# Three tables of places changed in the cross layers of a fused scan network on one Trainium2 core

## The chip, the cores and the metric

The kernel runs on one core of one Trainium2 chip. The metric is the device time of one execution in microseconds (us), lower is better. Its five engines run side by side, each its own instructions in order: TensorE (PE in the rows, PEld its weight loads), VectorE (DVE), ScalarE (ACT), GpSimd (POOL) and SyncE (SP), which here only issues DMAs. Semaphores order them among each other.

## The reference

The input x has shape (4, 32, 32, 96): 4 images, 1024 positions, 96 channels. Four layers follow each other, each as x = x + layer(group_norm(x)). Layers 0 and 3 (L0 and L3, the cross layers) are four-direction selective scans, layer 1 is a stencil of products ("motif"), layer 2 a one-direction selective scan behind a 3x3 convolution. The change touches only the code that L0 and L3 share. Cut to what matters, such a layer computes

```
xz = x @ in_proj.T                       # 2 x 192 channels: xin and z
xs = [rows order, columns order, and both reversed](xin)        # 4 directions
dts, Bs, Cs = x_proj[k] @ xs[k]          # ranks 12, 16, 16
delta = softplus(dt_proj[k] @ dts + bias)
h_t = exp(delta_t * A) * h_{t-1} + delta_t * B_t * u_t          # 16 states a channel
y   = sum over states of C_t * h_t + D * u
y   = layernorm over the 192 channels of the sum over directions
out = (y * silu(z)) @ out_proj.T
```

## The kernel before

A cross layer works through 8 turns, two for each of the 4 images: number 2b with the rows order (r = 0), number 2b + 1 with the columns order (r = 1). A turn has 48 tiles, indexed t = 0 to 47, in 16 groups g of three tiles: a group is one pair of states (states p and p + 8 on the two halves of the partitions) of one direction, its three tiles c = 0, 1, 2 are the three blocks of 64 of the 192 channels. Every tile is 128 x 1024.

One tile is: ACT takes the decay exp(delta * A) (L843); DVE multiplies du by the B row (L1007, "inject"; for c = 2 POOL does it, L897) and runs the scan (L1028); POOL multiplies the state by the C row (L910, "read"), with three read buffers; PE adds the two state halves into y_ps (L696). In each group ACT also copies the B row from SBUF to PSUM for the two DVE injects (L828, copy_b). It stands in front of the decay of the group's second tile.

SP loads the B and C rows of group g + 1 in iteration g of its loop (L568 and L577; load_c waits until POOL has read group g - 1). Beside that it makes the doubled copies of delta and du that a block of channels needs (copy_block, L549 and L550, four DMAs of 256 KB a block). Three blocks (q = 0, 1, 2, the first half of the next turn) are copied in the iterations that COPY_ABOVE lists, one row for r = 0 and one for r = 1; the other three at the iterations of COPY_BELOW. SP issues in order, so copies and what they wait for stand ahead of later row loads.

Between the tiles lie side products, which finish the image before (FINISH) and prepare the next turn (PREPARE). All go through a single PSUM bank side_ps, so a side product can't start before the one before it has been taken out. The tables give for each half of a side product (tile at which PE issues it, tile at which ACT takes it, tile at which DVE uses it). PE issues a side product ahead of the y addition of the tile with that index, ACT takes it behind the decay of its tile, DVE uses it ahead of the inject of its tile. The keys that matter:

- ("cent", j), the centred products: y minus its channel mean, for the layer norm. cent 0 has two halves of 4 matmuls in the trace, cent 1 is one product of 8 (lines L668 and L666). DVE multiplies the gate by it (L980), ACT squares it (L774) and so frees side_ps. They exist only in turns with r = 0 and b > 0: 3 turns in each of the two layers, 6 in all. Below, product 1, 2 and 3 are cent 0 half 0, cent 0 half 1 and cent 1.
- ("sum", j): the finished delta of block pair j, used by DVE (L976).

ACT_SOFTPLUS places the five ACT passes of the softplus for each j by tile: exp (L784), log (L789), one (L794), less (L797), relu (L800). Between less and relu comes the subtraction "gap" with both operands in SBUF, on POOL (L882) at tiles of POOL_GAP or on DVE (L994) at tiles of DVE_GAP. For j = 2 it is on DVE: tile 38 for r = 0, tile 33 for r = 1. At a given tile ACT does its decay first, then the takes, then the softplus passes. The copy_b of a group comes before the decay of its second tile.

Of the kernel before, what the change touches and what calls it, by code (L numbers as in the profile page):

```python
# [128 lines left out]
def motif_layer(nc, x_cm, g_cm, ident, cols, ahead):  # L129
# [5 lines left out]
    with cleared(nc) as (ctx, sems):  # L135
# [79 lines left out]
        def _(dve):  # L215
# [82 lines left out]
            for k in range(banks_out):  # L298
# [13 lines left out]


FINISH = [
    {("cent", 0): ((0, 5, 3), (2, 7, 6)),
     ("cent", 1): ((4, 9, 8),),
     ("var", 0): ((10, 14, None), (11, 15, None)),
     ("out", 0): ((14, None, 18), (15, None, 19))},
    {("z", 0): ((37, 40, None), (38, 41, None)),
# [22 lines left out]
     ("sum", 2): ((33, 37, 37), (36, 40, 39))}]  # L342
ACT_SOFTPLUS = [
    {("exp", 0): 23, ("log", 0): 23, ("one", 0): 25, ("less", 0): 25, ("exp", 1): 26, ("log", 1): 26,
     ("one", 1): 28, ("relu", 0): 29, ("less", 1): 31, ("relu", 1): 34, ("exp", 2): 36, ("log", 2): 36,
     ("one", 2): 36, ("less", 2): 36, ("relu", 2): 40},
    {("exp", 0): 16, ("log", 0): 16, ("one", 0): 18, ("less", 0): 20, ("relu", 0): 22, ("exp", 1): 25,
     ("log", 1): 27, ("one", 1): 27, ("less", 1): 29, ("exp", 2): 29, ("relu", 1): 31, ("log", 2): 31,
     ("one", 2): 31, ("less", 2): 31, ("relu", 2): 34}]
POOL_GAP = [{30: 1}, {20: 0, 27: 1}]  # L350
DVE_GAP = [{26: 0, 38: 2}, {33: 2}]
# [4 lines left out]
FILL, FILL_FIRST = 1, 2  # L356
FILL_AFTER = {(("var", 0), 1): 0, (("out", 0), 0): 0, (("out", 0), 1): 0, (("sum", 2), 1): 0,
              (("sum", 1), 0): 0}
COPY_BELOW, COPY_ABOVE = (1, 2, 3), ((13, 13, 15), (9, 9, 13))


def side_uses(r, finish):
# [1442 lines left out]
```

## Time and profile before

| what | value |
|---|---|
| median of 3 runs | 3565.45 us (3564.26 to 3565.74) |
| the profiled execution | 3555.9 us, span 3554.1 us |
| POOL busy / DVE busy | 2788.5 us (78%) / 3031.2 us (85%) |
| PE busy / ACT busy | 2451.9 us (69%) / 2049.0 us (58%) |
| reads L910 | 768 of 2387 ns mean |
| injects on POOL L897 | 256 of 2358 ns mean |
| scans L1028 | 768 in three groups of 2286, 2287 and 2271 ns mean |
| mean granted TensorE clock | 0.814 of full speed |

The profile is of one execution. A number in brackets behind an instruction is the idle time of its engine ahead of it, with the instruction or DMA that ended it. The time of a row is its start in us from the start of the span. In a chain of tiles an engine that is never idle sets the pace, and the idle time of the others costs nothing.

### The profile page before, as it was taken

To read this page: it belongs to the slowest core of one execution; us is meant where nothing else is said; L and a number is where in the kernel's file an instruction comes from. 1 tells how busy PE (TensorE), PEld (TensorE's weight loads), DVE (VectorE), ACT (ScalarE), POOL (GpSimd) and SP (SyncE) were. 2 spreads that over 40 slices of the span, in tenths; PEclk is the share of its full clock that TensorE was granted. 3 is DMA by queue.
4 is the path that set the end of the run, shared out by engine and by line. 5 is a ranking of instruction groups with operands and counts; after the bars stand their busy time and mean duration, and the time that the engine had idled before them with its cause. 6 is when DMAs were issued, how large, how long until landed. Compare 5 with 4: busy or idle time off the path is not lost. (4 is left out here: it accounts for less than half of the span.)

```text
span 3554.1 us, 27486 instructions
## 1 busy us (share of the span) xinstructions
PE 2451.9 (69%) x5948; PEld 618.1 (17%) x5948; DVE 3031.2 (85%) x1958; ACT 2049.0 (58%) x2262; POOL 2788.5 (78%) x1188
## 2 busy tenths in 40 slices
PE   5767676677677667335677776766776777768776
PEld 2111111111121111111111112111111111111111
DVE  1899999999999998685989841999999999999995
ACT  3566665757565665304656524657575656666564
POOL 0899999989998999003666622999899989999995
PEclk9787888879788878657788778778897888788788
DMA  2655556654755465103442402566537555655663
GB/s 49 160 138 145 140 136 157 153 131 116 180 132 142 124 155 127 30 0 90 120 106 80 119 11 68 145 161 149 141 111 178 140 136 125 159 136 136 148 152 91
DMA packets 140881, 437.19 MB, mean 123 GB/s; under 512 B 33909, under 2 KB 34619, under 8 KB 140395
## 3 DMA queue, kind: packets, MB, share of 16 engines
q1 hardware_dynamic: 140714, 435.58, 50.4%
q14 instruction: 137, 1.12, 0.1%
q8 instruction: 30, 0.49, 0.1%
HBM read 307.56 MB, written 6.82 MB: 88 GB/s over the span
## 5 line engine op out<-in xcount | busy, mean ns | idle before, releaser
L910 POOL TENSOR_TENSOR L_read<-L_state,L_c_rows 128x1024 f32<-128x1024 f32 x768 | 1818.7, 2387 | 115.9 <-DVE L_state L1028 70.5
L696 PE MATMUL L_y_ps<-L_read,L_fold 128*64 128x512 f32 x3072 | 990.5, 743 | 467.7 <-POOL L_read L910 467.5
L897 POOL TENSOR_TENSOR L_state<-L_du,L_b_rows 128x1024 f32<-128x1024 f32 x256 | 603.7, 2358 | 27.4 <-POOL L_read L910 4.1
L1028 DVE TENSOR_TENSOR_SCAN L_state<-L_decay,L_work_ps 128x1024 f32<-128x1024 f32 x256 | 585.3, 2286 | 27.7 <-DVE L_work_ps L1007 4.0
L843 ACT ACTIVATE L_decay<-L_delta,L_a_neg 128x1024 f32<-128x1024 f32 x512 | 584.1, 1141 | 16.1 <-DVE L_state L1028 9.2
L1028 DVE TENSOR_TENSOR_SCAN L_state<-L_decay,L_row_ps 128x1024 f32<-128x1024 f32 x256 | 585.4, 2287 | 8.8
L1028 DVE TENSOR_TENSOR_SCAN L_state<-L_work_ps,L_state 128x1024 f32<-128x1024 f32 x256 | 581.4, 2271 | 13.4 <-POOL L_state L897 8.2
L843 ACT ACTIVATE L_work_ps<-L_delta,L_a_neg 128x1024 f32<-128x1024 f32 x256 | 285.8, 1116 | 460.1 <-DVE L_state L1028 459.1
L1007 DVE TENSOR_TENSOR L_work_ps<-L_du,L_row_ps 128x1024 f32<-128x1024 f32 x256 | 314.3, 1228 | 196.2 <-issue 145.7
L696 PEld LDWEIGHTS L_y_ps<-L_read,L_fold 128*64 128x64 f32 x3072 | 183.4, 154 | 1214.7 <-POOL L_read L910 901.6
L1558 POOL TENSOR_TENSOR L_read<-L_state,L_c_rows 128x1024 f32<-128x1024 f32 x96 | 237.6, 2475 | 164.7 <-DVE L_state L1664 138.8
L828 ACT COPY L_row_ps<-L_b_rows 128x1024 f32<-128x1024 f32 x256 | 260.1, 1016 | 156.1 <-DVE L_state L1028 101.0
L1007 DVE TENSOR_TENSOR L_row_ps<-L_du,L_row_ps 128x1024 f32<-128x1024 f32 x256 | 309.4, 1208 | 0.0
L1664 DVE TENSOR_TENSOR_SCAN L_state<-L_decay,L_b_ps 128x1024 f32<-128x1024 f32 x96 | 219.5, 2286 | 3.3
L668 PE MATMUL L_side_ps<-g_cm,L_w_u 96*128 (+1 forms) x216 | 162.4, 843 | 44.9 <-ACTq L763 26.0
L668 PE MATMUL L_side_ps<-L_dbl,L_w_dt 128*128 128x512 f32 x216 | 142.6, 747 | 45.7 <-ACT L_delta L755 37.6
L1642 DVE TENSOR_TENSOR L_b_ps<-L_du,L_b_ps 128x1024 f32<-128x1024 f32 x96 | 117.2, 1221 | 59.8 <-DMA L_du<-L_du_a 41.8
L1354 PE MATMUL L_y_ps<-L_read,L_fold 128*64 128x512 f32 x384 | 126.3, 736 | 51.5 <-POOL L_read L1558 48.1
L1507 ACT ACTIVATE L_decay<-L_delta,L_a_neg 128x1024 f32<-128x1024 f32 x96 | 109.1, 1144 | 64.0 <-DVE L_state L1664 41.2
L1536 POOL TENSOR_TENSOR L_l_a<-L_more,L_l_a 128x1024 f32<-128x1024 f32 x4 | 9.4, 2362 | 169.7 <-ACT L_more L1436 169.6
L759 ACT COPY L_delta<-L_side_ps 128x512 f32<-128x512 f32 x108 | 62.7, 581 | 131.9 <-DVE L_u L976 55.6
L882 POOL TENSOR_TENSOR L_y_b<-L_more,L_y_b 128x1024 f32<-128x1024 f32 x10 | 23.5, 2354 | 121.7 <-ACT L_more L797 121.7
(326 smaller groups left out, 2933.5 us busy)
## 6 DMA issues: line engine op xcount, KB each, us to landing
L_b_rows<-L_bc_dram SPq DMA_DIRECT2D x580, 256.0 KB, 4.2
L_c_rows<-L_bc_dram SPq DMA_DIRECT2D x580, 256.0 KB, 4.0
L_delta<-L_delta SPq DMA_DIRECT2D x204, 256.0 KB, 5.2
L_du<-L_du SPq DMA_DIRECT2D x140, 256.0 KB, 5.6
L_du<-L_u SPq DMA_DIRECT2D x64, 256.0 KB, 6.0
L_bc_dram<-L_dbl SPq DMA_DIRECT2D x40, 128.0 KB, 3.4
L_delta<-L_delta_a SPq DMA_DIRECT2D x16, 256.0 KB, 4.4
L_du<-L_du_a SPq DMA_DIRECT2D x16, 256.0 KB, 5.0
```

Source lines behind the costliest of these rows:

```text
L668: m = nc.tensor.matmul(side_ps[0:rows, :], part[0], part[1], **flags)
L696: m = nc.tensor.matmul(y_to(c, o, i), fold[:, :], y_half(t, o, i), start=first, stop=last, skip_group_check=True)
L828: nc.scalar.copy(row_ps[:, :], b_rows[:, g % 2, :]).then_inc(b_ready, 1)
L843: nc.scalar.activation(to[:, :], delta2[:, d * NBLK + c, :], ACT.Exp, scale=a_neg[:, o * 2 + d, c, p:p + 1]).then_inc(decay_ready, 1)
L897: nc.gpsimd.tensor_tensor(state[:, last, :], du2[:, d * NBLK + last, :], b_rows[:, g % 2, :], ALU.mult).then_inc(injected_c, 1)
L910: nc.gpsimd.tensor_tensor(read[:, t % READS, :], state[:, t % STATES, :], c_rows[:, g % 2, :], ALU.mult).then_inc(multiplied, 1)
L1007: nc.vector.tensor_tensor(to[:, :], du2[:, d * NBLK + c, :], row_ps[:, :], ALU.mult).then_inc(injected, 1)
L1028: nc.vector.tensor_tensor_scan(state[:, c, way], by[:, way], fed[:, way], 0.0, ALU.mult, ALU.add).then_inc(scanned, 1)
L1354: m = nc.tensor.matmul(y_ps[quarter(i), c, :], fold[:, :], read[:, t % READS, s], start=t < NBLK, stop=t >= NT - NBLK, skip_group_check=True)
L1558: nc.gpsimd.tensor_tensor(read[:, t % READS, :], state[:, t % STATES, :], c_rows[:, p % 2, :], ALU.mult).then_inc(multiplied, 1)
L1642: nc.vector.tensor_tensor(to[:, :], du2[:, slot(number, c), :], row[:, :], ALU.mult).then_inc(injected, 1)
L1664: nc.vector.tensor_tensor_scan(state[:, t % STATES, :], decay[:, t % DECAYS, :], fed[:, :], 0.0, ALU.mult, ALU.add).then_inc(scanned, 1)
```

## The change

Three edits, all in tables of tile numbers; no instruction is added or removed, and both programs have the same number on each engine.

1. FINISH[0]: on PE product 1 goes from ahead of the y addition of tile 0 to ahead of that of tile 1, product 2 from tile 2 to tile 3; product 3 stays at 4. DVE uses product 1 at tile 4 instead of 3, product 3 at 7 instead of 8. ACT takes product 3 at tile 8 instead of 9.
2. ACT_SOFTPLUS, block pair j = 2: for r = 0 exp goes from tile 36 to 34, log to 35, one and less to 37; for r = 1 exp goes from 29 to 28 and log from 31 to 29.
3. COPY_ABOVE: for r = 0 from iterations (13, 13, 15) to (12, 13, 14), for r = 1 from (9, 9, 13) to (10, 11, 12).

```
-    {("cent", 0): ((0, 5, 3), (2, 7, 6)),
-     ("cent", 1): ((4, 9, 8),),
+    {("cent", 0): ((1, 5, 4), (3, 7, 6)),
+     ("cent", 1): ((4, 8, 7),),
...
-     ("one", 1): 28, ("relu", 0): 29, ("less", 1): 31, ("relu", 1): 34, ("exp", 2): 36, ("log", 2): 36,
-     ("one", 2): 36, ("less", 2): 36, ("relu", 2): 40},
+     ("one", 1): 28, ("relu", 0): 29, ("less", 1): 31, ("relu", 1): 34, ("exp", 2): 34, ("log", 2): 35,
+     ("one", 2): 37, ("less", 2): 37, ("relu", 2): 40},
     {("exp", 0): 16, ("log", 0): 16, ("one", 0): 18, ("less", 0): 20, ("relu", 0): 22, ("exp", 1): 25,
-     ("log", 1): 27, ("one", 1): 27, ("less", 1): 29, ("exp", 2): 29, ("relu", 1): 31, ("log", 2): 31,
+     ("log", 1): 27, ("one", 1): 27, ("exp", 2): 28, ("less", 1): 29, ("log", 2): 29, ("relu", 1): 31,
...
-COPY_BELOW, COPY_ABOVE = (1, 2, 3), ((13, 13, 15), (9, 9, 13))
+COPY_BELOW, COPY_ABOVE = (1, 2, 3), ((12, 13, 14), (10, 11, 12))
```

On PE, at the start of an r = 0 turn that finishes an image, before (the rows with L_cent_w and L_less_w are a centred product, L696 a y addition, L703 the skip term):

```order
L661 ISA
L668 MATMUL L_side_ps<-L_y_a,L_cent_w 128x512
L668 MATMUL L_side_ps<-L_y_b,L_less_w 128x512
L692 REGISTER_ALU
L693 ISA
L696 MATMUL L_y_ps<-L_read,L_fold 64x512 x2
L692 REGISTER_ALU
L693 REGISTER_ALU
L696 MATMUL L_y_ps<-L_read,L_fold 64x512 x2
L661 REGISTER_ALU
L668 MATMUL L_side_ps<-L_y_a,L_cent_w 128x512
L668 MATMUL L_side_ps<-L_y_b,L_less_w 128x512
```

and in the changed kernel, from the same place:

```order
L693 ISA
L696 MATMUL L_y_ps<-L_read,L_fold 64x512 x2
L649 REGISTER_ALU
L661 ISA
L668 MATMUL L_side_ps<-L_y_a,L_cent_w 128x512
L668 MATMUL L_side_ps<-L_y_b,L_less_w 128x512
L692 REGISTER_ALU
L693 REGISTER_ALU
L696 MATMUL L_y_ps<-L_read,L_fold 64x512 x2
L693 REGISTER_ALU
L696 MATMUL L_y_ps<-L_read,L_fold 64x512 x2
L703 MATMUL L_y_ps<-L_u,L_skip_diag 64x512 x2
```

Product 1 now stands behind the y addition of tile 0. Product 2, which waits for side_ps, no longer stands ahead of the y addition of tile 2.

On SP, in an r = 1 turn from iteration 9 on, before (L549 and L550 are the copies, L568 and L577 the B and C rows):

```order
L568 DMA L_b_rows<-L_bc_dram 64x1024 x2
L577 DMA L_c_rows<-L_bc_dram 64x1024 x2
L549 DMA L_delta<-L_delta 64x1024
L550 DMA L_du<-L_du 64x1024
L549 DMA L_delta<-L_delta 64x1024
L550 DMA L_du<-L_du 64x1024
L549 DMA L_delta<-L_delta 64x1024
L550 DMA L_du<-L_du 64x1024
L549 DMA L_delta<-L_delta 64x1024
L550 DMA L_du<-L_du 64x1024
L568 DMA L_b_rows<-L_bc_dram 64x1024 x2
L577 DMA L_c_rows<-L_bc_dram 64x1024 x2
```

and in the changed kernel, from the same iteration:

```order
L568 DMA L_b_rows<-L_bc_dram 64x1024 x2
L577 DMA L_c_rows<-L_bc_dram 64x1024 x2
L568 DMA L_b_rows<-L_bc_dram 64x1024 x2
L577 DMA L_c_rows<-L_bc_dram 64x1024 x2
L549 DMA L_delta<-L_delta 64x1024
L550 DMA L_du<-L_du 64x1024
L549 DMA L_delta<-L_delta 64x1024
L550 DMA L_du<-L_du 64x1024
L568 DMA L_b_rows<-L_bc_dram 64x1024 x2
L577 DMA L_c_rows<-L_bc_dram 64x1024 x2
```

The rows of group 11, the second pair here, no longer stand behind eight copies; one block of four copies follows them.

On ACT, in an r = 0 turn from the decay of tile 36 on, before (L843 is a decay, L828 copy_b of group 12, L759 takes a sum):

```order
L843 ACTIVATE L_decay<-L_delta,L_a_neg 128x1024
L784 ACTIVATE L_gate_a<-L_gate_a 128x1024
L789 ACTIVATE L_gate_b<-L_gate_a 128x1024
L794 ACTIVATE L_more<-L_gate_a 128x1024
L797 ACTIVATE L_more<-L_more,L_minus_col 128x1024
L828 COPY L_row_ps<-L_b_rows 128x1024
L843 ACTIVATE L_decay<-L_delta,L_a_neg 128x1024
L759 COPY L_delta<-L_side_ps 128x512
```

and in the changed kernel:

```order
L843 ACTIVATE L_decay<-L_delta,L_a_neg 128x1024
L828 COPY L_row_ps<-L_b_rows 128x1024
L843 ACTIVATE L_decay<-L_delta,L_a_neg 128x1024
L759 COPY L_delta<-L_side_ps 128x512
L794 ACTIVATE L_more<-L_gate_a 128x1024
L797 ACTIVATE L_more<-L_more,L_minus_col 128x1024
```

Nothing stands between the decay of tile 36 and copy_b of group 12 any more; two of the four passes are ahead of that decay and two behind the take of the sum.

## Rows read from the trace of the kernel before

**Rows 1.** The page, engines: busy us, share of the span, instructions.

```profile
PE 2451.9 (69%) x5948; PEld 618.1 (17%) x5948; DVE 3031.2 (85%) x1958; ACT 2049.0 (58%) x2262; POOL 2788.5 (78%) x1188
```

**Rows 2.** All waits: waiter <- ended by: us in total, times, longest.

```profile
POOL L_read L910 <- DVE L_state L1028: 70.5, 109, 1.7
ACT L_row_ps L828 <- DMA L_b_rows<-L_bc_dram: 52.5, 16, 3.9
POOL L_read L910 <- PE L_y_ps L696: 43.4, 27, 4.2
POOL L_state L897 <- DMA L_du<-L_du: 2.0, 3, 0.9
```

**Rows 3.** Stretches, groups 1 and 2 of six r = 0 turns: length, busy, clock, DMA.

```profile
770.50:796.56 26.06, 25.12 (x58) 5.02 (x58) 21.72 (x14) 13.25 (x16) 18.73 (x9) 0.66 0.69 161
...
sum 152.27, PE 146.53 PEld 29.74 DVE 127.31 ACT 79.24 POOL 112.52; mean PE 24.42 PEld 4.96 DVE 21.22 ACT 13.21 POOL 18.75
```

**Rows 4.** Stretches, groups 3 and 4 of the same six turns, their sum.

```profile
sum 112.62, PE 91.50 PEld 22.40 DVE 109.89 ACT 80.87 POOL 111.68; mean PE 15.25 PEld 3.73 DVE 18.31 ACT 13.48 POOL 18.61
```

**Rows 5.** Timeline of PE, start of a turn: start us, length, idle in brackets.

```profile
763.37 1.08 PE L696 MATMUL L_y_ps<-L_read,L_fold 128*64 128x512 f32 x4 [1.40 <-POOL L_read L910]
...
771.31 2.08 PE L668 MATMUL L_side_ps<-L_y_a,L_cent_w 128*128 128x512 f32 x2 [3.47 <-ACT L_sq_a L774]
...
775.32 1.98 PE L696 MATMUL L_y_ps<-L_read,L_fold 128*64 128x512 f32 x4
...
782.93 1.97 PE L666 MATMUL L_side_ps<-L_y_a,L_less_w 128*64 128x512 f32 x4
...
786.74 1.86 PE L696 MATMUL L_y_ps<-L_read,L_fold 128*64 128x512 f32 x4
```

**Rows 6.** Timeline of POOL in the same stretch.

```profile
777.45 2.35 POOL L910 TENSOR_TENSOR L_read<-L_state,L_c_rows 128x1024 f32<-128x1024 f32 x1 [1.98 <-PE L_y_ps L696]
...
788.75 2.36 POOL L910 TENSOR_TENSOR L_read<-L_state,L_c_rows 128x1024 f32<-128x1024 f32 x1 [4.22 <-PE L_y_ps L696]
...
796.56 2.37 POOL L910 TENSOR_TENSOR L_read<-L_state,L_c_rows 128x1024 f32<-128x1024 f32 x1
```

**Rows 7.** Timeline of DVE in the same stretch.

```profile
767.30 2.29 DVE L1028 TENSOR_TENSOR_SCAN L_state<-L_decay,L_work_ps 128x1024 f32<-128x1024 f32 x1
...
786.86 0.69 DVE L980 TENSOR_TENSOR L_gate_b<-L_gate_b,L_side_ps 128x512 f32<-128x512 f32 x1 [3.75 <-PE L_side_ps L666]
```

**Rows 8.** Stretches of that turn, columns as in rows 3; the clock follows POOL.

```profile
759.00:764.40 5.40, 3.23 (x10) 0.79 (x8) 5.37 (x4) 3.86 (x5) 5.27 (x3) 1.00 0.72 190
764.40:788.30 23.90, 19.01 (x38) 3.35 (x36) 19.63 (x14) 9.28 (x11) 17.73 (x8) 0.50 0.68 159
```

**Rows 9.** Timeline of SP in an r = 1 turn, iterations 9 and 10.

```profile
688.83 0.48 SPq L549 DMA_DIRECT2D L_delta<-L_delta  x1
...
697.25 2.30 SPq L568 DMA_DIRECT2D L_b_rows<-L_bc_dram  x2
```

**Rows 10.** Timeline of ACT in that turn, tile 34.

```profile
703.27 1.02 ACT L828 COPY L_row_ps<-L_b_rows 128x1024 f32<-128x1024 f32 x1 [3.56 <-DMA L_b_rows<-L_bc_dram]
```

**Rows 11.** Timeline of DVE in that turn, tile 33.

```profile
700.16 2.73 DVE L994 TENSOR_TENSOR L_gate_b<-L_more,L_gate_b 128x1024 f32<-128x1024 f32 x1
704.41 1.23 DVE L1007 TENSOR_TENSOR L_work_ps<-L_du,L_row_ps 128x1024 f32<-128x1024 f32 x1 [1.52 <-ACT L_row_ps L828]
```

**Rows 12.** Timeline of POOL in that turn: inject of group 11, tiles 33 and 34.

```profile
705.18 2.36 POOL L897 TENSOR_TENSOR L_state<-L_du,L_b_rows 128x1024 f32<-128x1024 f32 x1
...
712.17 4.67 POOL L910 TENSOR_TENSOR L_read<-L_state,L_c_rows 128x1024 f32<-128x1024 f32 x2 [1.67 <-DVE L_state L1028]
```

**Rows 13.** Timeline of DVE in an r = 0 turn, tiles 36 and 38.

```profile
882.67 1.23 DVE L1007 TENSOR_TENSOR L_work_ps<-L_du,L_row_ps 128x1024 f32<-128x1024 f32 x1 [1.33 <-ACT L_row_ps L828]
...
889.68 1.20 DVE L994 TENSOR_TENSOR L_gate_b<-L_more,L_gate_b 128x1024 f32<-128x1024 f32 x1
```

**Rows 14.** Timeline of POOL in that turn, tiles 36 to 38.

```profile
887.07 2.36 POOL L910 TENSOR_TENSOR L_read<-L_state,L_c_rows 128x1024 f32<-128x1024 f32 x1
889.84 5.68 POOL L910 TENSOR_TENSOR L_read<-L_state,L_c_rows 128x1024 f32<-128x1024 f32 x2 [0.40 <-DVE L_state L1028]
```

## The prediction

> **What bounds the kernel now.** I read the page first, then the list of all waits, then the stretches of single groups, and last the timelines of three places. On the page DVE and POOL are busiest [rows 1], and neither is saturated over the span. In the cross layers POOL sets the pace. A group costs it one inject and three reads, 4 x 2.35 = 9.4 us by the durations of [rows 6, 12]. In undisturbed groups that is all: groups 3 and 4 of six turns take 112.62 us, 18.77 a turn, with POOL busy 111.68 of it and DVE 109.89 [rows 4]. So DVE has only 2% of slack, and anything that it does on top of a group comes out as time. What can be won is POOL's idle time in these layers: 70.5 us in which it waits for a scan and 43.4 us in which it waits for PE [rows 2]. The question for each edit is how much of that it takes away.
>
> **Edit 1, centred products (six turns).** Groups 1 and 2 of these turns take 152.27 us, 25.4 a turn, against the 18.77 of undisturbed ones [rows 3, 4]. All of these six turns lose alike. The timeline shows how. PE runs the y addition of tile 0 at 763.37; product 2, which stands ahead of the y addition of tile 2, then waits 3.47 us until ACT has taken product 1 [rows 5]. The y addition of tile 2 comes out only at 775.32 + 1.98 = 777.3, and POOL, whose read of tile 5 needs that buffer, has waited 1.98 us for it [rows 5, 6]. From 764.4 to 788.3 the granted clock is 0.50, that is 1.2 GHz, and PE works off a backlog: a y addition takes 1.98 us, against 1.08 at full clock, and product 2 with its two parts 775.32 - 771.31 = 4.0 us [rows 5, 8]. So product 3 is done only at 786.7; DVE waited 3.75 us for it at tile 8, and POOL 4.22 us for the y addition behind it [rows 5 to 7].
>
> After the change PE is given work as it arrives. Product 1 follows the y addition of tile 0. At half clock, which I take for these two since PE now has nothing between 759 and 763.4, that is 763.4 + 2.0 + 4.0 = 769.4. The y additions of tiles 1 and 2 follow without a wait, done by 773.2. DVE has one product less ahead of tile 3: its scan, at 767.30 before [rows 7], ends 0.6 us earlier, at 769.0. I add the DVE chain with 0.6 a product, 1.24 an inject, 2.2 a scan: product 1 to 770.0, tile 4 to 773.5, tile 5 to 775.7, product 2 to 776.3, tile 6 to 779.8, product 3 to 780.4, tile 7 to 783.9, tile 8 to 786.1. POOL: reads of tiles 4 and 5 start at 773.5 and 775.9, the inject of group 2 at 778.2, reads of tiles 6 to 8 at 780.6, 783.9 and 786.3, the inject of group 3 at 788.6, the next read at 791.0, where it was 796.56 [rows 6]. That is 20.5 us for the two groups. The same from the other side: 18.77 plus three products of 0.69 [rows 7] is 20.8. The part of the chain that I can't see is PE: product 2 can start at about 775 if the first skip term also ran at half clock, and then ends 1.3 to 3 us behind what DVE asks. I take 0.4 us for it, so 21.2 a turn. Cost after: 6 x 21.2 = 127.2; **gain 152.3 - 127.2 = 25 us**. Bounds: 6 x 20.6 gives a gain of 29; and a loss of 14.5, if the clock stays at half (rival 2).
>
> The clock decides how much of it comes, so it is weighed on its own. The row shows that PE had 3.23 us of work in 5.40 before its clock fell, then stood idle up to 771.31, and from there it was busy without a pause and still at 0.50 up to 788.3 [rows 5, 8]. Most of that work fills only half of the array (128 x 64 twice, 64 x 64 twice). What I expect: the y addition, product 1 and two y additions in one run, without the pause, bring the clock back sooner. The Trainium skill (TensorE: Matmul & The Clock Gate, section "What's actually happening") says that idling halves the clock and that sustained activity gives it back. By that rule product 2 runs at full clock in every turn, and the gain is the 29 us. The trace agrees on the fall, and not on the return: it didn't come in 17 us of unbroken work.
>
> **Edit 3, copies of the first half.** In r = 1 turns SP holds the B row of group 11 behind eight copies, which wait until 688.83 for delta and then occupy the queue up to 697.25 [rows 9]. The row lands at 703.2: ACT had waited 3.56 us for it [rows 10], and DVE's inject of tile 33 started at 704.41, 1.52 us after the subtraction ended [rows 11]. The list has 16 such waits with 52.5 us, two a pair of turns [rows 2]. After the change the load stands ahead of the copies, so it is out before 688.83, over 8 us earlier. ACT's copy_b then is done before DVE's subtraction ends, and DVE goes on at 700.16 + 2.73 = 702.9. POOL meanwhile is held by its own inject, 705.18 to 707.5 [rows 12], so the read of tile 33 gains little; the read of tile 34, which waited 1.67 for DVE [rows 12], comes the full 1.5 earlier. Behind it DVE stays the later one by some tenths, so 1.5 stays. Eight turns: **gain 12 us**. What is queued behind the moved copies: at iterations 10 to 12 each block of four DMAs holds the next B row for half of 697.25 - 688.83, some 4 us [rows 9]. The waits for B rows stand at group 11 of r = 1 and group 15 of r = 0, eight each, behind double blocks; the single blocks of COPY_BELOW have none. So I count nothing. Bounds: 0, if another wait stands behind it, and 8 x 1.67 = 13.4.
>
> For r = 0 the copies go from (13, 13, 15) to (12, 13, 14). The other eight of the 16 waits are for group 15, where DVE had a sum to do, so nobody waited. The last block lands earlier, which takes away POOL's wait for du at the start of the r = 1 turns, 2.0 us in three of them [rows 2]. **Gain 2 us**, bounds 0 and 2.
>
> **Edit 2, softplus passes.** For r = 0 four passes of about 1.05 us stood ahead of copy_b of group 12, and DVE waited 1.33 us for it at tile 36 [rows 13]. That wait goes. But little comes of it. The read of tile 36 is POOL's own pace, without a wait, and that of tile 37 waited only 0.40 [rows 14]. And DVE's subtraction, which took 1.20 us because it began right behind a read [rows 13], now begins about 1.3 us earlier, inside the read at 887.07. In the r = 1 turn the same subtraction began inside a read, took 2.73, and the next reads took longer [rows 11]. It so ends at 889.4 + 1.1 = 890.6 against 890.9. I take 0.25 us in eight turns: **gain 2 us**, bounds 0 and 8 x 1.33 = 11. The Trainium skill (SBUF — State Buffer, section "Who interferes with whom") has the rule: a DVE operation with two SBUF inputs and a GpSimd operation exclude each other, and the later one waits for the end of the other. The trace agrees, with 2.73 against 1.20. Without that rule the gain would be nearer 0.4 x 8 = 3 us, so it costs this edit one or two. For r = 1 the two passes move in time that ACT spends waiting: nothing.
>
> **The sum.** 25 + 12 + 2 + 2 = 41 us off the profiled execution's 3555.9: 3514.9. The median of the runs shown lies 9.55 us above that execution, so the forecast is 3565.45 - 41 = 3524.5 us.
>
> **Rivals.**
> 1. Half of edit 1: the clock comes back, but in some turns only behind product 2. Then DVE waits 2 to 3 us in half of them. For it: the start of each turn lies otherwise against the chip's changes of clock. Gain of edit 1 about 12: 3537.
> 2. Half clock through the whole start of the turn, as before. Then PE ends product 1 at 769.4, tiles 1 and 2 with the skip term at 775.1, product 2 at 779.2, the next y and skip at 783, product 3 at 786.9, as late as before, and DVE has the inject and the scan of tile 7 behind it as well as the scan of tile 8. Scan 7 ends at 791.2, scan 8 at 793.5, the read of group 3 starts at 798.3: 27.8 us for the two groups, 6 x 27.8 - 152.3 = 14.5 lost. With 16 from the rest: 3564. For it: 0.50 in all of 764.4 to 788.3 [rows 8].
> 3. Slower: the same place, DVE's use of product 3 at tile 7 instead of 8, at its upper price. Product 1 at half clock is 1.9 us longer than before, when it ran at full; if that passes down the backlog whole, a turn loses (27.8 - 25.4) + 1.9 = 4.3, six turns 26, less 16: 3575. It decides from 3.9 us a turn on (16 + 7.1 over 6). Against it: it needs half clock and no slack in PE's queue, and the pause of 3.47 us is gone.
> 4. The copies only move the wait: SP's queue delays another row, edit 3 gives nothing: 3537. Against it: after the change no iteration has more than four copies, and the list has no wait behind such an iteration.
>
> **How the numbers follow.** Forecast 0.70, rival 1 0.12, rival 2 0.08, rival 3 0.04, rival 4 0.06. About 0.2% (7 us) is what a measurement of this kernel can tell from no change. Faster: 0.70 + 0.12 + 0.06 = 0.88; within 0.2%, rival 2: 0.08; slower, rival 3: 0.04. The forecast's own range is 3515 to 3535: 29 instead of 25 at one end, half of edit 3 missing at the other, and some us for turns that meet the clock otherwise. The range for 8 in 10 takes in rivals 1 and 4: 3512 to 3546.
>
> **What would show it.** Edit 1: groups 1 and 2 of the six turns at about 21 us instead of 25.4; POOL's waits for PE down from 43.4 us to under 15; the granted clock there above 0.8. Edit 3: no wait of ACT for L_b_rows before tile 34, inject of tile 33 right behind the subtraction. Edit 2: no wait ahead of the inject of tile 36, and a subtraction at tile 38 that takes over 2 us. Wrong would be: DVE waiting over 2 us for product 2 or 3, or the B rows of groups 12 to 14 landing behind ACT's need.

## The result

| kernel | median | lowest to highest | ratio to before, 95% interval |
|---|---|---|---|
| before | 3565.45 us | 3564.26 to 3565.74 | |
| changed | 3525.59 us | 3524.31 to 3532.5 | 0.9898, 0.9884 to 0.9912 |

The changed kernel is 39.9 us faster by the medians; the forecast was 41. The two profiled executions, of 3555.9 and 3524.3 us, are only 31.6 us apart: the one of before lay 9.5 us below its runs, the one of the changed kernel was the fastest of its own. Executions of one kernel scatter by some us (24 of the kernel before, on another occasion, went from 3552.7 to 3573.0; three of all those below, with 3633, 3893 and 5033 us, lie far outside and do not count in the ratios). So below, times are compared by medians of one occasion, and parts of the change by the length of the same groups in two traces, summed over all turns. A group lasts here from the start of POOL's read of its first tile to that of the next group.

### The profile after

The page, engines, the row that answers to [rows 1]. All busy times but DVE's and PE's stay within 3 us.

```profile
PE 2433.4 (69%) x5948; PEld 616.9 (18%) x5948; DVE 3036.4 (86%) x1958; ACT 2051.4 (58%) x2262; POOL 2788.5 (79%) x1188
```

All waits of the changed kernel, against [rows 2]: waiter <- ended by: us in total, times, longest.

```profile
POOL L_read L910 <- DVE L_state L1028: 75.3, 108, 1.8
...
DVE L_work_ps L1007 <- ACT L_row_ps L828: 22.1, 20, 3.1
...
POOL L_read L910 <- PE L_y_ps L696: 5.1, 8, 1.2
```

POOL's waits for PE fell from 43.4 us to 5.1. The two DMA rows of [rows 2], 52.5 us of ACT for B rows and 2.0 of POOL for du, are gone. New in size is DVE's longest wait for copy_b, 3.1 us. The list of before has

```profile
DVE L_work_ps L1007 <- ACT L_row_ps L828: 39.2, 38, 1.8
```

Stretches of the changed kernel, the same as in [rows 3]: groups 1 and 2 of the six r = 0 turns that finish an image, the second of them and the sum. The columns are start and end, length, busy time of PE, PEld, DVE, ACT and POOL with the number of instructions, granted clock, busy share of the DMA engines and GB/s. The sum is 122.50 instead of 152.27, with the clock at 0.94 in this turn instead of 0.66.

```profile
762.19:783.13 20.94, 18.31 (x60) 4.07 (x56) 20.07 (x14) 12.05 (x14) 18.70 (x10) 0.94 0.91 204
...
sum 122.50, PE 103.62 PEld 22.85 DVE 118.96 ACT 71.72 POOL 112.17; mean PE 17.27 PEld 3.81 DVE 19.83 ACT 11.95 POOL 18.69
```

Stretches of the start of that turn, against [rows 8]. Half clock lasts 10.3 us instead of 23.9.

```profile
752.50:754.40 1.90, 0.00 (x0) 0.00 (x0) 1.86 (x2) 1.25 (x2) 1.90 (x2) 1.00 0.40 93
754.40:764.70 10.30, 9.83 (x18) 2.35 (x20) 10.04 (x7) 4.77 (x5) 9.75 (x5) 0.50 0.49 124
764.70:783.10 18.40, 15.77 (x54) 3.54 (x50) 17.56 (x13) 10.68 (x12) 16.32 (x7) 1.00 0.89 200
```

PE in that turn, against [rows 5]. Group 1 begins 8.3 us earlier than in before's trace, the y addition of tile 0 8.5 us.

```profile
754.87 1.98 PE L696 MATMUL L_y_ps<-L_read,L_fold 128*64 128x512 f32 x4 [4.30 <-POOL L_read L910]
756.78 2.08 PE L668 MATMUL L_side_ps<-L_y_a,L_cent_w 128*128 128x512 f32 x2
...
760.79 3.68 PE L696 MATMUL L_y_ps<-L_read,L_fold 128*64 128x512 f32 x8
...
765.50 1.13 PE L668 MATMUL L_side_ps<-L_y_a,L_cent_w 128*128 128x512 f32 x2
...
769.62 1.08 PE L666 MATMUL L_side_ps<-L_y_a,L_less_w 128*64 128x512 f32 x4
```

Product 1 runs at half clock (2.08 us for what takes 1.13 later), the y additions of tiles 1 and 2 follow without a pause, the clock is back at 764.7, and products 2 and 3 run at full speed. DVE in that turn, its three uses of the products, against [rows 7]:

```profile
760.89 0.69 DVE L980 TENSOR_TENSOR L_gate_a<-L_gate_a,L_side_ps 128x512 f32<-128x512 f32 x1
...
767.72 0.69 DVE L980 TENSOR_TENSOR L_gate_a<-L_gate_a,L_side_ps 128x512 f32<-128x512 f32 x1 [0.49 <-PE L_side_ps L668]
...
771.87 0.66 DVE L980 TENSOR_TENSOR L_gate_b<-L_gate_b,L_side_ps 128x512 f32<-128x512 f32 x1
```

Only the second waits, 0.49 us, and the wait of 3.75 at the third is gone. In all six turns no use of a product waits longer than 0.76 us.

Groups 10 and 11 of the eight r = 1 turns, sums of the stretches, before and then the changed kernel:

```profile
sum 177.03, PE 116.98 PEld 35.66 DVE 161.90 ACT 81.85 POOL 157.29; mean PE 14.62 PEld 4.46 DVE 20.24 ACT 10.23 POOL 19.66
```

```profile
sum 163.90, PE 111.70 PEld 32.21 DVE 161.47 ACT 81.84 POOL 157.14; mean PE 13.96 PEld 4.03 DVE 20.18 ACT 10.23 POOL 19.64
```

That is 13.1 us less. DVE in the same place as [rows 11]: the inject now stands right behind the subtraction.

```profile
689.93 2.66 DVE L994 TENSOR_TENSOR L_gate_b<-L_more,L_gate_b 128x1024 f32<-128x1024 f32 x1
692.52 1.22 DVE L1007 TENSOR_TENSOR L_work_ps<-L_du,L_row_ps 128x1024 f32<-128x1024 f32 x1
```

Two places give time back. In groups 5 and 6 of the six r = 0 turns, 125.77 us became 130.54. POOL waits there for a scan of DVE, which it did not in before's trace:

```profile
814.39 4.67 POOL L910 TENSOR_TENSOR L_read<-L_state,L_c_rows 128x1024 f32<-128x1024 f32 x2 [0.71 <-DVE L_state L1028]
```

And in groups 13 to 15 of the r = 1 turns, 241.59 became 251.41. The stretches of the changed kernel there, their sum:

```profile
sum 251.41, PE 182.31 PEld 38.84 DVE 222.08 ACT 160.74 POOL 219.66; mean PE 22.79 PEld 4.85 DVE 27.76 ACT 20.09 POOL 27.46
```

It comes from three of the eight turns (3, 11 and 15, counting all turns of both layers from 0), which lose 9.9 us together and look alike. Turn 3, first PE from 713.4 on, then ACT, then DVE at tile 42:

```profile
713.40:726.30 12.90, 12.75 (x20) 2.90 (x20) 9.65 (x6) 5.97 (x8) 12.40 (x6) 0.50 0.51 127
```

```profile
723.48 0.58 ACT L769 COPY L_gate_b<-L_side_ps 64x512 f32<-64x512 f32 x1 [2.27 <-PE L_side_ps L668]
723.97 1.01 ACT L828 COPY L_row_ps<-L_b_rows 128x1024 f32<-128x1024 f32 x1
```

```profile
725.10 1.23 DVE L1007 TENSOR_TENSOR L_work_ps<-L_du,L_row_ps 128x1024 f32<-128x1024 f32 x1 [3.09 <-ACT L_row_ps L828]
```

PE is at half clock and behind, ACT takes the second half of the z product late, and copy_b of group 14, which stands behind that take, comes 3.09 us late for DVE.

### The profile page after: what moved, and what is told of

Its sections match the earlier page's. It is cut to its first block and busy times, and to the rows that moved or that the text cites. A ratio compares the mean times of both kernels' runs of the same rounds, so it can differ in the third digit from the quotient of the medians.

```text
span 3522.5 us, 27486 instructions
## 1 busy us (share of the span) xinstructions
PE 2433.4 (69%) x5948; PEld 616.9 (18%) x5948; DVE 3036.4 (86%) x1958; ACT 2051.4 (58%) x2262; POOL 2788.5 (79%) x1188
## 3 DMA queue, kind: packets, MB, share of 16 engines
q14 instruction: 137, 1.12, 0.1%
## 5 line engine op out<-in xcount | busy, mean ns | idle before, releaser
L696 PE MATMUL L_y_ps<-L_read,L_fold 128*64 128x512 f32 x3072 | 998.3, 749 | 466.3 <-POOL L_read L910 466.1
L843 ACT ACTIVATE L_decay<-L_delta,L_a_neg 128x1024 f32<-128x1024 f32 x512 | 583.9, 1140 | 15.7 <-DVE L_state L1028 9.5
L843 ACT ACTIVATE L_work_ps<-L_delta,L_a_neg 128x1024 f32<-128x1024 f32 x256 | 285.7, 1116 | 440.4 <-DVE L_state L1028 439.3
L696 PEld LDWEIGHTS L_y_ps<-L_read,L_fold 128*64 128x64 f32 x3072 | 186.6, 157 | 1219.9 <-POOL L_read L910 913.4
L828 ACT COPY L_row_ps<-L_b_rows 128x1024 f32<-128x1024 f32 x256 | 260.0, 1016 | 130.9 <-DVE L_state L1028 127.9
L759 ACT COPY L_delta<-L_side_ps 128x512 f32<-128x512 f32 x108 | 62.9, 582 | 153.6 <-DVE L_du L976 66.6
L668 PE MATMUL L_side_ps<-L_delta,ident 128*128 128x512 f32 x216 | 123.8, 657 | 0.0
```

The costliest lines, as they stand in the source:

```text
L668: m = nc.tensor.matmul(side_ps[0:rows, :], part[0], part[1], **flags)
L696: m = nc.tensor.matmul(y_to(c, o, i), fold[:, :], y_half(t, o, i), start=first, stop=last, skip_group_check=True)
L828: nc.scalar.copy(row_ps[:, :], b_rows[:, g % 2, :]).then_inc(b_ready, 1)
L843: nc.scalar.activation(to[:, :], delta2[:, d * NBLK + c, :], ACT.Exp, scale=a_neg[:, o * 2 + d, c, p:p + 1]).then_inc(decay_ready, 1)
```

## The experiments

Group lengths are differences to the trace of before unless another kernel is named. Half clock means a granted clock of 0.50.

### One edit at a time

**cent_only**: the two FINISH lines of the change, the rest as before.

```
-    {("cent", 0): ((0, 5, 3), (2, 7, 6)),
-     ("cent", 1): ((4, 9, 8),),
+    {("cent", 0): ((1, 5, 4), (3, 7, 6)),
+     ("cent", 1): ((4, 8, 7),),
```

> The kernel before with edit 1 alone (centred products at the new places). Theory (PE's wait for the side bank ahead of the y addition of tile 2 starts the backlog): groups 1 and 2 of the six turns fall from 25.4 to 20 to 21 us each, POOL's waits for PE from 43 to about 5 us; 25 to 30 us off, 3536 to 3541. Rival (most of the changed kernel's gain comes from the copies, and edit 1 only moves a wait of POOL from PE to DVE): groups 1 and 2 stay over 23 us a turn, less than 15 us off, over 3550.

Measured 3537.93 us beside 3559.5 of before, ratio 0.9944 (0.9927 to 0.996): 21.6 us. The time is inside the expected 3536 to 3541, the gain below the expected 25 to 30. Its waits:

```profile
POOL L_read L910 <- DVE L_state L1028: 87.5, 122, 2.0
...
ACT L_row_ps L828 <- DMA L_b_rows<-L_bc_dram: 52.5, 16, 3.9
...
POOL L_read L910 <- PE L_y_ps L696: 6.0, 9, 1.7
```

The waits for PE go with this edit, those for B rows stay, and POOL's waits for DVE rise from 70.5 to 87.5: part of what PE no longer costs is then set by DVE. Groups 1 and 2 gain 27.5 us, groups 5 and 6 give 5.6 back.

**copies_only**: the COPY_ABOVE line of the change.

```
-COPY_BELOW, COPY_ABOVE = (1, 2, 3), ((13, 13, 15), (9, 9, 13))
+COPY_BELOW, COPY_ABOVE = (1, 2, 3), ((12, 13, 14), (10, 11, 12))
```

> The kernel before with edit 3 alone (both rows of the first-half copies). Theory (the B row of group 11 stands behind eight copies): the wait of ACT for it, 3.6 us in each of eight r = 1 turns, goes, groups 10 and 11 lose 1.5 us a turn, group 15 of the r = 0 turns 0.3 to 0.5; 14 to 17 us off, 3549 to 3551. Rival (ACT's softplus passes of block pair 2 were the cause, and without edit 2 ACT is late for tile 34 all the same): under 5 us off.

Measured 3546.53 us, ratio 0.997 (0.9954 to 0.9986), 13.0 us, where 14 to 17 were expected. Its runs went from 3537.0 to 3560.7, wider than any gain at stake here; the groups say it more sharply. Groups 10 and 11 of r = 1 lose 13.2 us, group 15 of r = 0 loses 4.0, groups 1 and 2 gain no time (1.7 us longer). Its sum of the stretches of groups 10 and 11:

```profile
sum 163.84, PE 119.15 PEld 35.35 DVE 160.92 ACT 81.83 POOL 157.03; mean PE 14.89 PEld 4.42 DVE 20.11 ACT 10.23 POOL 19.63
```

**copies_r1**: the same for r = 1 alone.

```
-COPY_BELOW, COPY_ABOVE = (1, 2, 3), ((13, 13, 15), (9, 9, 13))
+COPY_BELOW, COPY_ABOVE = (1, 2, 3), ((13, 13, 15), (10, 11, 12))
```

> Edit 3 for the r = 1 turns alone, iterations (10, 11, 12) instead of (9, 9, 13), r = 0 as before. Theory: all of the 12 to 13 us of groups 10 and 11 come from here, and r = 0 adds only the start of the r = 1 turns: 12 us off, 3553, and 2 to 4 us above the kernel with both. Rival (it is the load on the DMA queues in both turns): half of it, 3558.

Measured 3557.46 us, 0.9986 (0.9973 to 1.0), 2.0 us off instead of the expected 12, with eight of ten runs in two clusters, 3543 to 3546 and 3557 to 3560: the time decides nothing. Its trace is of the slowest, 3565.7. Groups 10 and 11 are shorter by 13.2 us there too, but groups 13 to 15 longer by 7.0 (248.60 against 241.59), with the 3.1 us wait at tile 42 in two turns. The 16 turns together are 1.2 us shorter than in before's trace; what makes this execution long lies outside them, 11 us more, where no edit touches anything. So edit 3 alone brings the gain in both traces, and the loss behind it in one of the two: copies_only, with the whole edit, has 240.33 us in groups 13 to 15.

**softplus_only**: the ACT_SOFTPLUS lines of the change, shortened here, r = 0 and then r = 1.

```
-     ... ("exp", 2): 36, ("log", 2): 36,
-     ("one", 2): 36, ("less", 2): 36, ...
+     ... ("exp", 2): 34, ("log", 2): 35,
+     ("one", 2): 37, ("less", 2): 37, ...
...
-     ... ("less", 1): 29, ("exp", 2): 29, ("relu", 1): 31, ("log", 2): 31,
+     ... ("exp", 2): 28, ("less", 1): 29, ("log", 2): 29, ("relu", 1): 31,
```

> The kernel before with edit 2 alone. Theory (the earlier subtraction begins inside a read of POOL and waits for its end, so the freed wait of 1.33 us comes to 0.25 us a turn; r = 1 gets nothing): 2 us off, 3563, group 12 of r = 0 turns 0.2 to 0.4 us shorter, the subtraction at tile 38 over 2 us long instead of 1.2. Rival (the wait of DVE of 1.33 us at tile 36 is on the path): 8 x 1.33 = 11 us off, 3555.

Measured 3560.95 us, ratio 1.0007 (0.9994 to 1.0019): no difference in the time. The trace shows where the gain stops. All subtractions of line 994 on L_gate_b in this kernel, least/median/most ns, which in before were 1199/1824/2893:

```profile
L994 DVE TENSOR_TENSOR L_gate_b<-L_more,L_gate_b x16: 2037/2412/2880, 230.8 to 3463.1; 128x1024 f32<-128x1024 f32 x16
```

None is short any more: DVE comes 1.3 us earlier in the r = 0 turns and meets POOL's read. Group 12 of all eight r = 0 turns goes from 86.11 to 83.85 us, 2.3 less, which the time can't tell from nothing.

### Which part of edit 1 brings it

A second occasion, before at 3563.6 us. **after_again** is the changed kernel once more.

> The changed kernel itself, beside the others of this call. Theory (parts add up: edit 1 about 22, edit 3 about 13, edit 2 about 2): 36 to 41 us below the kernel before. Rival (the new waits of DVE at tile 42 of three r = 1 turns, 10 us in the first trace, come from the copies at iterations 11 and 12 and stand in every execution): they are there again in r = 1 turns 3, 7 and 8 of the eight. By the theory they follow the clock and stand in other turns, or in fewer.

Measured 3526.28 us, ratio 0.99 (0.9883 to 0.9916), 37.3 us, as expected. Groups 1 and 2 take 20.1 to 21.1 us in each turn, and the 3.1 us waits at tile 42 are there again, but in turns 7 and 11 instead of 3, 11 and 15 (the second, sixth and eighth r = 1 turn; the expectation above miscounts them). They are no property of a turn.

**cent_pe**: PE's new places, ACT and DVE as before. The diff is against the changed kernel.

```
-    {("cent", 0): ((1, 5, 4), (3, 7, 6)),
-     ("cent", 1): ((4, 8, 7),),
+    {("cent", 0): ((1, 5, 3), (3, 7, 6)),
+     ("cent", 1): ((4, 9, 8),),
```

> The changed kernel with PE's order of the centred products, but DVE's and ACT's places as before: product 1 used by DVE at tile 3, product 3 at DVE tile 8 and ACT tile 9. Theory (PE's order is what removes the backlog, and DVE's later place for product 1 is its complement): DVE waits 2 to 3.5 us at tile 3 for product 1, which PE now issues behind the y addition of tile 0; groups 0 to 2 about 2 to 3 us a turn longer than in the changed kernel, 12 to 18 us, still shorter than before. Rival (DVE's and ACT's places did nothing): same as the changed kernel.

Measured 3539.1 us, ratio 0.9934 (0.9912 to 0.9956), 12.8 us slower than after_again. DVE comes for product 1 at tile 3 and waits 2.3 to 3.8 us in the six turns, 3.10 on average, so group 0 becomes 13.9 us longer in sum (72.78 against 58.93). Groups 1 and 2 lose only 19.1 us instead of 29.8. Groups 5 and 6 take 126.26 us, nearly as before. PE's move needs DVE's to follow.

**cent_dve**: DVE's and ACT's new places, PE as before.

```
-    {("cent", 0): ((1, 5, 4), (3, 7, 6)),
+    {("cent", 0): ((0, 5, 4), (2, 7, 6)),
```

> The changed kernel with DVE's and ACT's places new, but PE's order as before: products at PE tiles 0, 2 and 4. Theory (product 2 ahead of the y addition of tile 2 waits for the side bank and starts the backlog): groups 1 and 2 stay at 24.5 to 28 us a turn, at half clock, POOL waits for PE over 30 us in all, 20 to 35 us above the changed kernel. Rival (DVE's wait for product 3 was the loss, and its new place removes it): groups 1 and 2 under 22.5 us.

Measured 3563.2 us, ratio 0.9999 (0.9987 to 1.001), 36.9 us above after_again where 20 to 35 were expected: all of the change's gain is gone. Groups 1 and 2, one turn and the sum, columns as in [rows 3]:

```profile
768.99:796.19 27.20, 24.40 (x58) 5.02 (x58) 19.90 (x14) 12.12 (x14) 18.70 (x9) 0.70 0.69 157
...
sum 163.11, PE 148.63 PEld 29.98 DVE 119.44 ACT 72.78 POOL 112.28; mean PE 24.77 PEld 5.00 DVE 19.91 ACT 12.13 POOL 18.71
```

And its waits:

```profile
POOL L_read L910 <- DVE L_state L1028: 103.0, 109, 6.6
DVE L_gate_b L980 <- PE L_side_ps L666: 47.3, 8, 6.9
```

With product 2 ahead of the y addition of tile 2, PE is late at half clock, and DVE, which now wants product 3 at tile 7, waits up to 6.9 us for it: 27.2 us a turn, 10.8 us more than before in sum. POOL's waits for PE came to 17.0 us, not the expected 30 and more: POOL is held by DVE instead, 103.0 us. This is the state of rivals 2 and 3, produced by another order of PE. Groups 5 and 6 take 130.45 us here, as in the changed kernel.

**cent_p2**: as the changed kernel, but product 1 back at tile 0. Product 2 keeps its new place.

```
-    {("cent", 0): ((1, 5, 4), (3, 7, 6)),
+    {("cent", 0): ((0, 5, 4), (3, 7, 6)),
```

> The changed kernel with product 1 back at PE tile 0 and product 2 at tile 3: only product 2 moves. Theory A (it is enough that the y addition of tile 2 is not held): groups 1 and 2 at 20 to 21.5 us, time as the changed kernel. Theory B (the unbroken run of y addition, product 1 and two y additions is needed to bring the clock back): PE then idles before product 2, the clock stays at half up to the end of group 2 in most of the six turns, product 3 is late, groups 1 and 2 at 22.5 to 25 us, 12 to 20 us above the changed kernel.

Measured 3545.46 us, ratio 0.9951 (0.9928 to 0.9975), 19.2 us slower than after_again. Groups 1 and 2, two of the six turns and the sum:

```profile
768.13:792.63 24.50, 22.86 (x49) 4.54 (x46) 20.00 (x14) 12.11 (x14) 18.71 (x9) 0.64 0.76 171
1095.91:1115.76 19.85, 15.16 (x50) 3.54 (x50) 19.47 (x14) 11.71 (x13) 18.68 (x9) 1.00 0.96 214
...
sum 138.63, PE 122.36 PEld 25.15 DVE 119.36 ACT 71.41 POOL 112.22; mean PE 20.39 PEld 4.19 DVE 19.89 ACT 11.90 POOL 18.70
```

One kernel shows both cases, with the same instructions: 24.5 us in the four turns that have half clock in their first 13.6 to 14.8 us, 19.85 and 20.78 in the two others. PE's timeline of the slow turn and of the fast one:

```profile
757.41 1.12 PE L668 MATMUL L_side_ps<-L_y_a,L_cent_w 128*128 128x512 f32 x2 [0.77 <-ACT L_y_b L819]
...
763.47 1.97 PE L696 MATMUL L_y_ps<-L_read,L_fold 128*64 128x512 f32 x4 [1.57 <-POOL L_read L910]
...
769.59 2.07 PE L668 MATMUL L_side_ps<-L_y_a,L_cent_w 128*128 128x512 f32 x2
...
1086.10 2.07 PE L668 MATMUL L_side_ps<-L_y_a,L_cent_w 128*128 128x512 f32 x2 [0.77 <-ACT L_y_b L819]
...
1095.96 1.12 PE L668 MATMUL L_side_ps<-L_y_a,L_cent_w 128*128 128x512 f32 x2 [0.32 <-ACT L_sq_a L774]
```

In the four slow turns product 1 still got full clock (1.12 us), the y additions behind it came with pauses, the clock fell there, and product 2 ran slow. In the turn of 19.85 us product 1 ran at half clock and product 2 fast. The turn of 20.78 us is neither: products 1 and 2 both got full clock, and the clock fell only within product 3. In all twelve turns of the changed kernel's two traces product 1 began at half clock (1.79 to 2.08 us for its first two matmuls), product 2 got full clock, and groups 1 and 2 took 20.1 to 21.1 us. So what the move of product 1 brings is a start at half clock, early, where nobody waits for it, and work without a pause behind it. The start alone is not enough: in cent_pe product 1 began at half clock in all six turns too, PE then paused 1.6 to 3.1 us ahead of product 2, and nearly all of product 2 ran at half clock. Product 1's move with product 2 left at tile 2 was not run.

### What is given back in r = 1, and how to have it

A third occasion, before at 3557.32 us, all three on top of the changed kernel. Each changes the r = 1 table only.

**sum2_earlier**: the second half of the finished delta of j = 2 is taken by ACT at tile 39 and used by DVE at tile 38.

```
-     ("sum", 2): ((33, 37, 37), (36, 40, 39))}]
+     ("sum", 2): ((33, 37, 37), (36, 39, 38))}]
```

> The changed kernel with the second half of the last sum in r = 1 turns used by DVE at tile 38 instead of 39 and taken by ACT at tile 39 instead of 40. In two or three r = 1 turns of the changed kernel PE works at half clock from tile 39 to 42, ACT takes a z product late, and copy_b of group 14 and DVE's inject of tile 42 wait 3.1 us. Theory (PE's pause of 2.4 us ahead of the first z product lets the clock fall there, and an earlier sum takes the pause away): the waits of 3.1 us go in all eight turns, groups 13 to 15 lose 5 to 10 us in all, 3517 to 3522. Rival (the clock falls there whatever PE does in that pause): 3526, same as the changed kernel.

Measured 3523.08 us, ratio 0.9894 (0.9874 to 0.9914), where 3517 to 3522 was expected; the interval takes in the changed kernel's ratio. All 3.1 us waits are gone, and groups 13 to 15 take 243.27 instead of 251.41 us. But group 12 costs 5.5 us more, and group 8, which the edit doesn't touch, 2.4 more (it goes from 80.8 to 84.5 us in the traces with this table there). It moves the loss.

**sum0_later**: DVE uses the first half of the finished delta of j = 0 at tile 26 instead of 25.

```
-     ("sum", 0): ((22, 27, 25), (25, 30, 29)),
+     ("sum", 0): ((22, 27, 26), (25, 30, 29)),
```

> The changed kernel with the first half of sum 0 in r = 1 turns used by DVE at tile 26 instead of 25. DVE waits 2.2 us for PE there in each of the eight turns, POOL 0.8. Theory (DVE does tile 25 in the time that it waited): POOL's 0.8 us at tile 25 goes, 5 to 8 us off in eight turns, 3519 to 3521. Rival (PE's next side product waits for that use, so the wait comes back at the second half or at the u product): within 2 us of the changed kernel.

Measured 3510.69 us, ratio 0.9865 (0.9844 to 0.9886): the fastest of all, 14.9 us below the changed kernel's first median and by the two ratios 12, more than was expected. Group 8 of the eight r = 1 turns, the changed kernel and then this one:

```profile
sum 81.81, PE 60.96 PEld 17.86 DVE 80.05 ACT 55.44 POOL 74.86; mean PE 7.62 PEld 2.23 DVE 10.01 ACT 6.93 POOL 9.36
```

```profile
sum 75.21, PE 52.99 PEld 17.52 DVE 63.31 ACT 58.91 POOL 74.45; mean PE 6.62 PEld 2.19 DVE 7.91 ACT 7.36 POOL 9.31
```

POOL is busy 74.45 of 75.21 us now, so that place is at its pace. The wait that went, in both lists (in before it was 17.8, 11, 2.5):

```profile
DVE L_du L976 <- PE L_side_ps L668: 19.4, 13, 2.5
```

```profile
DVE L_du L976 <- PE L_side_ps L668: 2.9, 7, 0.5
```

That is 6.6 us, by the mechanism and inside the expected 5 to 8. Most of the rest of the lead in this trace lies in groups 13 to 15, 240.71 against 251.41, where no 3.1 us wait occurred. **sum_both** has the two edits together.

> Both of the other two edits of this call on top of the changed kernel. Theory: they add up, 10 to 16 us below the changed kernel, 3510 to 3516, and it is the fastest of all. Rival (each takes away slack that the other needs, or the clock comes out otherwise): no faster than the better of the two.

Measured 3522.05 us, ratio 0.9893 (0.9874 to 0.9912). It was expected to be the fastest at 3510 to 3516, and it is 11 us slower than sum0_later. Group 8 gains 6.6 us again, group 12 loses 5.6 and groups 13 to 15 take 243.24: as groups the parts add up, 8 us above sum0_later's, so the earlier sum 2 isn't worth its price. Why its time is only 1 us below sum2_earlier's stays open.

**sum0_again**, a fourth occasion, before at 3559.61 us, is sum0_later once more.

> The same kernel as sum0_later, once more on another occasion. Theory (8 us come from group 8, the rest from z products that don't fall into half clock because they lie otherwise against the clock): median 3507 to 3517, ratio to the kernel before 0.985 to 0.988, no wait of 3.1 us at tile 42 in r = 1 turns, or one at most. Rival (the first trace had luck with the clock): the waits of 3.1 us are back in two or three turns, 3518 to 3522.

Measured 3513.78 us, ratio 0.9868 (0.9849 to 0.9886), so the lead over the changed kernel holds. But the 3.1 us waits are back, in turns 11 and 15, as the rival had it. The 6.5 us of group 8 are there, the absence of the waits in the first trace was chance. By the ratios the lead is 11 us; what brings the part beyond group 8 isn't shown.

## Why the prediction was right

The forecast of 3524.5 us met the median of 3525.59. For edit 1 the mechanism was right. That the number came so close is in part luck: by group lengths the edits bring 34.7 of the 41 us, and the runs lie 39.9 us apart. Step by step:

- **Edit 1, the chain of a turn.** Shifted by the 8.3 us by which group 1 starts earlier, the forecast had product 1 done on PE at 761.1, the y additions of tiles 1 and 2 at 764.9, the uses of the three products done at 761.7, 768.0 and 772.1. The rows have 760.8, 764.5, and 761.6, 768.4 and 772.5. The allowance of 0.4 us for product 2 was a wait of 0.49. The six turns took 20.4 us on average where 21.2 was forecast, a gain of 29.8 in groups 1 and 2 instead of 25, just above the upper bound of 29.
- **What was missed in it.** POOL waits for DVE at another place: groups 5 and 6 took 4.8 us more, 5.6 in cent_only. Net it is the 25 us of the forecast, by two errors that cancel, which is luck. The range of edit 1 did not contain that second term. It comes with the new places of DVE and ACT: cent_dve has it (130.45 us) though its groups 1 and 2 are the slowest of all, and cent_pe, with DVE's and ACT's old places, has 126.26. Through which wait those places act on groups 5 and 6 isn't shown.
- **The clock.** The forecast said that one run without the pause of 3.47 us brings it back sooner, and it came back at 764.7, before product 2. The Trainium skill (TensorE: Matmul & The Clock Gate, section "What's actually happening") says that sustained activity returns the full clock. The rows agree for this run, and by that rule the forecast had product 2 at full clock in every turn, which is what all twelve turns show. But there are busy stretches without a return: from 713.4 to 726.3 of the changed kernel PE was busy 12.75 of 12.90 us at 0.50 throughout. One reading of the forecast was wrong and bore no number: PE did not stand idle from the fall of the clock to 771.31. It did the y addition of tile 1 at half clock in between, and only the last 3.47 us were idle:

```profile
765.86 1.98 PE L696 MATMUL L_y_ps<-L_read,L_fold 128*64 128x512 f32 x4 [1.42 <-POOL L_read L910]
```

- **Edit 3, r = 1.** 12 us forecast, 13.1 measured in groups 10 and 11, 13.2 in each kernel that has the edit alone. ACT's wait for the B row is gone, as forecast.
- **Edit 3, what it gives back.** The forecast counted nothing behind the moved copies. Groups 13 to 15 of r = 1 took 9.8 us more, 8.5 in after_again, 7.0 in copies_r1. The three traces without the edit have none of the 3.1 us waits (241.59 before, 239.9 in cent_only, 242.2 in softplus_only). Of the nine with it and sum 2 at its old place seven have them, and two don't: copies_only (240.33) and sum0_later (240.71). So that the edit causes the loss isn't shown. The forecast named a late B row as what would prove it wrong; it was PE at half clock and ACT's take of z ahead of copy_b. Which turns meet that stays open: it moved from turn to turn between executions of one kernel.
- **Edit 3, r = 0.** 2 us forecast with 2 as the upper bound, 4.1 measured: group 15 takes 77.72 instead of 81.85 us in all eight turns, 9.6 to 9.8 a turn instead of 9.8 to 10.6. The forecast had counted only the three waits for du.
- **Edit 2.** 2 us forecast, 2.3 measured in group 12, nothing in the time. The subtraction at tile 38 took 1.84 to 2.28 us instead of 1.20, because it now meets a read. That is the rule of the Trainium skill (SBUF — State Buffer, section "Who interferes with whom") as the forecast used it, and the rows agree: in this turn it begins at 876.18, inside the read that began at 875.01, and ends at 878.43, 1.1 us after 877.36, where a read of 2.35 us ends.
- **The rivals.** Rival 1 (half of edit 1) is what cent_p2 shows: four turns of six with the clock back only late. Rivals 2 and 3 worked out 27.8 us a turn with product 3 late and used at tile 7; cent_dve has 27.2. It lost 10.8 us in these groups where rival 2 had 14.5. Neither happened to the change, because both of PE's moves were in it. Rival 4 did not occur: no row was late.

The terms add up by group lengths: six r = 0 turns -28.8, the two others -2.0, the eight r = 1 turns -3.9, together -34.7. By edits that is 25.0 for edit 1, 13.1 - 9.8 + 4.1 = 7.4 for edit 3 and 2.3 for edit 2, against 41 forecast: the term that was too large is edit 3. With +3.1 outside the turns the difference of spans is -31.6. The median of the runs says -39.9. In pieces, 21.6 + 13.0 - 1.5 = 33 us by the single edits. Two things explain part of the distance. The 16 turns of after_again take 2576.8 us against 2616.5 in before's trace, 39.6 less, so the turns of one kernel scatter by 5 us. And what lies outside the turns goes from 937.6 to 948.7 us over the 14 traces, though no edit touches it, with before's trace the shortest. No trace of a median execution of before is there to settle the rest.

## What to carry to other kernels

When a side product is moved, move its producer and its consumer together, and then write down which consumer is next in line on each engine: here moving PE's places alone cost 12.8 of the 37.3 us, and moving DVE's and ACT's alone all of them. In a chain that is 2% from its bound a new place can also cost time in groups further on (5 us here), so read the groups after the place as well as the place itself. For single edits of a few us the length of the same groups in two traces decides; the time of a run carries a scatter larger than the edit.

## What the runs showed of the hardware

- One program shows two speeds at one place with the granted clock: in cent_p2 19.85 us with the clock at 1.00 and 24.50 at 0.64, with the same instructions. What came just before differs: a product at half clock followed by unbroken work, or a product at full clock followed by pauses of 1.24 and 1.57 us. The third kind of turn (20.78 us) shows that a product at full clock can also be followed by a second one at full clock.
- PE held at 0.50 while fully busy, 12.75 of 12.90 us in the changed kernel; in before 17 us of unbroken work [rows 5, 8]. In the changed kernel it came back after 10.3 us, 9.83 of them busy.
- A DVE subtraction of two SBUF operands of 128 x 1024 takes 1.20 us when it begins just before a POOL read (the eight r = 0 turns of before), and 2.0 to 2.9 us in all 16 cases of softplus_only. POOL pays in either case: in all 32 subtractions of these two traces the POOL read that begins during it takes 3.2 to 3.4 us instead of 2.35, so an earlier or later place of the subtraction doesn't save that.
